# An AdaLN block whose query projection becomes three split products, with GpSimd and VectorE making the low halves

## What is computed

```python
mod = (_silu(L0_c) @ L0_wmod).reshape(L0_c.shape[0], 6, 1, -1)
sa, ca, ga, sb, cb, gb = (mod[:, 0], ..., mod[:, 5])
ga = (2 * (ga >= 0) - 1) * jnp.maximum(jnp.abs(ga), 0.25)        # gb alike
h = _layernorm(x, axis=-1) * (1 + ca) + sa
Q = jnp.einsum('bsh,hd->bsd', h, Wq) + bq                         # K = V = Q
scores = jnp.einsum('bqh,bkh->bqk', Q, K) / jnp.sqrt(128)
x = x + ga * jnp.einsum('bqk,bkh->bqh', softmax(scores), V)
h = _layernorm(x, axis=-1) * (1 + cb) + sb
# route = sigmoid(h @ Wr + br); out = max(route) * gelu(h @ W1[e]) @ W2[e], e = argmax(route)
x = x + gb * ffn(h)
```

## Time and profile before

| | us |
|---|---|
| median of 3 timed runs | 354.4 (354.29 to 354.92) |
| the profiled execution, device time | 354.34 |
| its span in the profile | 352.6 |
| busy share of the span | PE 92%, DVE 79%, ACT 63%, POOL 55% |
| attention slots 3 to 12 | 11.75 each |
| attention slots 1, 2, 13, 14 | 11.89, 12.61, 13.50, 12.96 |

### The profile page before, as it was taken

How to read it: one execution, slowest core, us unless ns; L and a number is a source line. 1 busy time by engine, 2 the same in 40 slices (tenths; PEclk the granted TensorE clock), 3 DMA queues, 4 the chain that set the end, 5 groups by cost and what they waited for, 6 DMA issues and landing times.

```text
span 352.6 us, 8419 instructions
## 1 busy us (share of the span) xinstructions
PE 325.0 (92%) x2578; PEld 299.6 (85%) x2578; DVE 278.9 (79%) x1114; ACT 223.5 (63%) x477; POOL 193.1 (55%) x224
## 2 busy tenths in 40 slices
PE   2799999999999999999989898899999999999960
PEld 2388788889888988898878798899999999999960
DVE  5378898898889888988997896899897777877730
ACT  2589987888788878887866585654445454434320
POOL 5016467545754575457525445877566556565661
PEclk9999999999999999999999999999999999999995
DMA  3394124337653666943536612664989554454300
GB/s 113 116 256 104 44 68 131 100 112 121 146 105 104 123 128 188 249 138 111 105 91 224 231 50 87 186 205 134 289 259 307 166 171 120 127 139 125 93 21 4
DMA packets 34493, 49.27 MB, mean 140 GB/s; under 512 B 4320, under 2 KB 26115, under 8 KB 34448
## 3 DMA queue, kind: packets, MB, share of 16 engines
q1 hardware_dynamic: 27504, 31.74, 37.0%
q0 software_dynamic: 6368, 16.92, 12.9%
q10 hardware_dynamic: 576, 0.07, 0.1%
HBM read 28.21 MB, written 20.96 MB: 139 GB/s over the span
## 4 chain that ended last, share of the span: by engine, by line
PE 70%; DVE 13%; ACT 6%; issue 5%; DVEq 2%; DMA 1%; POOL 1%; POOLq 0%; SPq 0%; ACTq 0%
PE mixed L625 14%; PE mixed L525 12%; PE flipped L512 6%; PE side L479 4%; PE scores L502 3%; PE scores L500 3%; PE scores L501 3%; PE side L545 3%; PE side L469 2%; PE scores L609 2%; PE scores L610 2%; PE scores L608 2%; PE side L537 2%; PE side L487 2%; PE flipped L609 2%
## 5 line engine op out<-in xcount | busy, mean ns | idle before, releaser
L1406 POOL DMA_INDIRECT sorted_rows<-payload,slots x64 | 63.9, 998 | 79.8 <-DVE slots L1044 64.9
L1433 POOL DMA_INDIRECT out_dram<-y_out,tokens x71 | 74.9, 1055 | 42.4 <-DVE y_out L1105 25.8
L625 PE MATMUL mixed<-down_slot,hidden 128*128 128x128 f32 x568 | 70.1, 276 | 2.5 <-ACT hidden L804 2.5
L625 PEld LDWEIGHTS mixed<-down_slot,hidden 128*128 128x128 f32 x568 | 66.5, 192 | 3.0 <-ACT hidden L804 3.0
L525 PE MATMUL mixed<-v_sb,probs_t 128*128 128x128 f32 x512 | 69.0, 278 | 0.0
L747 ACT ACTIVATE probs<-scores,row_max 128x512 f32<-128x512 f32 x64 | 44.0, 687 | 35.1 <-DVE row_max L937 33.4
L525 PEld LDWEIGHTS mixed<-v_sb,probs_t 128*128 128x128 f32 x512 | 62.2, 192 | 0.2
L937 DVE TENSOR_REDUCE row_max<-scores 128x1 f32<-128x512 f32 x64 | 44.1, 688 | 19.0 <-PE scores L502 19.0
L789 ACT ACTIVATE f_hi<-side 128x256 fp32r<-128x256 f32 (+1 forms) x39 | 14.3, 366 | 42.8 <-PE side L587 42.8
L512 PE MATMUL flipped<-ident,probs 128*128 128x128 f32 x256 | 39.1, 275 | 0.4 <-ACT probs L747 0.3
L755 ACT ACTIVATE probs_t<-flipped 128x512 f32<-128x512 f32 x64 | 37.9, 594 | 0.0
(11 more groups left out here) (187 smaller groups left out, 768.7 us busy)
## 6 DMA issues: line engine op xcount, KB each, us to landing
rows<-sorted_rows SPq DMA_DIRECT2D x32, 388.0 KB, 3.7
x_tile<-in_L_attn_inputs_dram SPq DMA_DIRECT2D x16, 256.0 KB, 3.2
payload<-stored_gates SPq DMA_DIRECT2D x16, 256.0 KB, 9.3
sorted_rows<-pad_rows SPq DMA_DIRECT2D x9, 388.0 KB, 4.6
w_parts<-in_L_ffn_W_dram SPq DMA_DIRECT2D x1, 2048.0 KB, 8.8
rows<-sorted_rows SPq DMA_DIRECT2D x7, 194.0 KB, 2.6
out_dram<-y_out,tokens POOLq DMA_INDIRECT x71
gate<-stored_gates SPq DMA_DIRECT2D x16, 64.0 KB, 5.8
```

What stands on the lines that cost most here:

```text
L625: last = nc.tensor.matmul(mixed[t % 2][:, u * H:(u + 1) * H], hidden[:, t % 2, f, u * P:(u + 1) * P], down_slot[:, t % 3, f, :], start=(f ...
L1406: nc.gpsimd.indirect_dma_start(rows_dram, bass.IndirectOffsetOnAxis(ap=slots[:, c:c + 1], axis=0), payload[:, b.q, j, :], None).then_inc(s ...
L1433: nc.gpsimd.indirect_dma_start(out_rows, bass.IndirectOffsetOnAxis(ap=tokens[:, t % RING, u:u + 1], axis=0), y_out[:, t % RING, u, :], Non ...
```

## The change

- `project` no longer takes h_t and wq_sb. ScalarE's `input_t` writes h_hi, which is scale * xn rounded to fp32r, without the shift. A new `split_h` on VectorE reads the same PSUM bank and makes h_lo = scale * xn - h_hi. TensorE then adds three fp32r products: wq_lo with h_hi, wq_hi with h_lo, wq_hi with h_hi.
- The halves of Wq are made once: wq_hi by ScalarE, wq_lo by VectorE. The shift is multiplied with Wq once for all batches (a small float32 product of 16 columns into mixed0) and becomes part of q_bias, one column for each batch, made by VectorE.
- Both outputs of `query` now have the factor ROOT and the same bias, so q_lo = q_t - q_hi is a plain subtraction. It moves from VectorE to GpSimd, as the first step of GpSimd's slot, for all batches but the first, which VectorE does in slot -1 (`split_first_q`). V, which is made from q_t, is put right by a factor 1/ROOT in the gates; for this two of the four gate instructions of the start are each written as two of half the width.
- In TensorE's slot `project(after)` moves behind `score(now, 2)`. In VectorE's slot `split_h(after)` is second, right behind `find_max(now, 1)`, and `split_q(after)` is gone from its place in front of `find_max(now, 3)`.

```diff
@@ TensorE
-                pe.wait_ge(h_ready, b.n + 1)
                 if b.n == 0:
                     pe.wait_ge(s_small, 64)
-                nc.tensor.matmul(side[1][:], wq_sb[:], h_t[:], start=True, stop=True).then_inc(q_projected, 1)
+                    pe.wait_ge(s_dve0, 3)
+                    nc.tensor.matmul(mixed[0][:, 0:B], wq_sb[:], shift1[:], start=True, stop=True
+                                     ).then_inc(bias_product, 1)
+                    pe.wait_ge(wq_split, 1)
+                pe.wait_ge(h_split, b.n + 1)
+                nc.tensor.matmul(side[1][:], wq_lo[:], h_hi[:], start=True, stop=False)
+                nc.tensor.matmul(side[1][:], wq_hi[:], h_lo[:], start=False, stop=False)
+                nc.tensor.matmul(side[1][:], wq_hi[:], h_hi[:], start=False, stop=True).then_inc(q_projected, 1)
...
                 mix(before, 3)
+                score(now, 2)
                 project(after)
                 if ending:
                     flip_rows(0)
-                score(now, 2)
@@ ScalarE
+            act.wait_ge(s_small, 64)
+            nc.scalar.activation(wq_hi[:], wq_sb[:], ACT.Copy).then_inc(wq_half, 1)
...
-                nc.scalar.activation(h_t[:], side[1][:], ACT.Identity, bias=shift1[:, col],
-                                     scale=scale1[:, col]).then_inc(h_ready, 1)
+                nc.scalar.activation(h_hi[:], side[1][:], ACT.Identity, scale=scale1[:, col]).then_inc(h_ready, 1)
...
-                nc.scalar.activation(q_t[:, b.p, :], side[1][:], ACT.Identity, bias=bq_sb[:, 0:1]
+                col = slice(b.n, b.n + 1)
+                nc.scalar.activation(q_t[:, b.p, :], side[1][:], ACT.Identity, bias=q_bias[:, col], scale=ROOT
                                      ).then_inc(q_ready, 1)
@@ VectorE
+            dve.wait_ge(wq_half, 1)
+            nc.vector.tensor_sub(wq_lo[:], wq_sb[:], wq_hi[:].bitcast(F32)).then_inc(wq_split, 1)
+            dve.wait_ge(bias_product, 1)
+            nc.vector.tensor_scalar(q_bias[:], mixed[0][:, 0:B], bq_sb[:, 0:1], ROOT, ALU.add, ALU.mult
+                                    ).then_inc(bias_ready, 1)
+            def split_h(b):
+                dve.wait_ge(h_ready, b.n + 1)
+                nc.vector.scalar_tensor_tensor(h_lo[:], side[1][:], scale1[:, col], h_hi[:].bitcast(F32),
+                                               ALU.mult, ALU.subtract).then_inc(h_split, 1)
...
                 find_max(now, 1)
+                split_h(after)
                 residual(before, 2)
...
-                split_q(after)
+                if k == -1:
+                    split_first_q()
@@ GpSimd
+            def split_q(b):
+                if not real(b) or b.n == 0:
+                    return
+                pool.wait_ge(q_hi_ready, b.n + 1)
+                nc.gpsimd.tensor_sub(q_lo[:, b.p, :], q_t[:, b.p, :], q_hi[:, b.p, :].bitcast(F32)).then_inc(q_split, 1)
...
             def slot(k):
+                split_q(after)
                 invert1(after2)
                 invert2(before)
                 token_ids(before2)
```

More of the change, by code:

```diff
@@ L85, in adaln_block @@
         bq_sb = sb("bq_sb", [P, 1])
-        bq_root = sb("bq_root", [P, 1])
+        q_bias = sb("q_bias", [P, B])
+        wq_hi = sb("wq_hi", [P, H], F32R)
+        wq_lo = sb("wq_lo", [P, H], F32R)
         wr_sb = sb("wr_sb", [P, E])
@@ L122, in adaln_block @@
         xn = sb("xn", [P, J, H])
-        h_t = sb("h_t", [P, J * P])
+        h_hi = sb("h_hi", [P, J * P], F32R)
+        h_lo = sb("h_lo", [P, J * P], F32R)
         q_t = sb("q_t", [P, 2, J * P])
@@ L237, in adaln_block @@
         xn_flipped = sem("xn_flipped")
+        wq_half = sem("wq_half")
+        wq_split = sem("wq_split")
+        bias_product = sem("bias_product")
         h_ready = sem("h_ready")
+        h_split = sem("h_split")
         q_projected = sem("q_projected")
@@ L729, in query @@
                 if b.n == 0:
-                    act.wait_ge(s_small, 64)
+                    act.wait_ge(bias_ready, 1)
                 wait(act, q_split, b.n - 1)
                 wait(act, v_ready, b.n - 1)
-                nc.scalar.activation(q_t[:, b.p, :], side[1][:], ACT.Identity, bias=bq_sb[:, 0:1]
+                col = slice(b.n, b.n + 1)
+                nc.scalar.activation(q_t[:, b.p, :], side[1][:], ACT.Identity, bias=q_bias[:, col], scale=ROOT
                                      ).then_inc(q_ready, 1)
-                if b.n == 0:
-                    act.wait_ge(bias_ready, 1)
-                nc.scalar.activation(q_hi[:, b.p, :], side[1][:], ACT.Identity, bias=bq_root[:, 0:1], scale=ROOT
+                nc.scalar.activation(q_hi[:, b.p, :], side[1][:], ACT.Identity, bias=q_bias[:, col], scale=ROOT
                                      ).then_inc(q_hi_ready, 1)
@@ L1416, in slot @@
             def slot(k):
-                before2, before, after2 = batch_at(k - 2), batch_at(k - 1), batch_at(k + 2)
+                before2, before, after, after2 = (batch_at(k + d) for d in (-2, -1, 1, 2))
+                split_q(after)
                 invert1(after2)
```

20 lines of the change are left out of this document (11 added, 9 removed).

## The result

The changed kernel takes **359.67 us** (median of 4 runs, 359.07 to 359.81), the kernel before 354.54 beside it (4 runs): a ratio of 1.0137, 95% interval 1.012 to 1.0153. It is 5 us slower. The forecast of 355.7 and its range up to 358.6 missed; the time is near that of Rival 2 (359.2). The profiled execution took 359.58 us with a span of 357.8, against 352.6 before.

A forecast was written before the change was run, and what follows sets the result against it. TensorE bounds ten slots of 11.75 us; after the change a loop through GpSimd and VectorE takes over. 354.34 + 0.6 (start) + 1.0 (slots 1 and 2) + 0.0 (ten slots) - 0.2 (end) = 355.7 us, range 353.4 to 358.6.

The forecast's parts named there:

- Rival 2: VectorE's `var` is held while GpSimd subtracts: 0.35 us a slot, +3.5 over ten slots, 359.2 us in all; chance 0.10.
- TensorE's slot without another bound: Steady slots 3 to 12: three fp32r products replace the float32 projection, so TensorE's slot falls by 0.18 to 11.58 us.
- Loop through GpSimd: Steady slots: `slots`, scatter, split, powers, normalize2 and back grow from 10.76 to 11.76 us, giving back TensorE's whole gain.
- `var` held, ten slots: VectorE in slots 3 to 12: no hold of `var` by GpSimd's subtraction, so 0; +3.5 us if held.
- Split on GpSimd: GpSimd's 128x512 subtraction for q_lo takes 1.28 us, like L1412, with bounds 1.01 and 1.56.
- h_lo on VectorE, start to start: VectorE's new h_lo takes 0.60 us, within 0.55 and 0.75, and stands on no binding path.
- Slots 1 and 2: GpSimd is already late there, so rstd2 comes later: +0.6 and +0.4, together +1.0 us, bounds 0 and +1.8.
- Start: First projection waits for VectorE's gates, wq_lo, q_bias and h_lo, ending at 14.3: +0.6 us, bounds +0.2 and +1.2.
- Slot 13: Full on VectorE with the same count of instructions: zero change.
- Slot 14: TensorE's saving reaches `find_max`: -0.2 us.
- the forecast case: GpSimd's loop sets the steady slot, within 0.08 us of 11.76: 355.7 us, own range 354.8 to 356.9; chance 0.45.

The follow-up runs named there:

- low parts on VectorE: Changed kernel with all q_lo made by VectorE again, in front of find_max(now, 3); 354.63 us against 354.66 for the kernel before, ratio 0.9997.
- reduction: Changed kernel with `var` written as a sum over one element instead of an addition, EPS left out of the second norm; 356.61 us, ratio 1.0046.
- the repetition: The changed kernel measured once more with nothing altered; 359.56 us against 354.66 for the kernel before, ratio 1.013.
- split in the middle: Changed kernel with GpSimd's order altered to second norm's power, q's subtraction, first norm's power; 365.52 us, ratio 1.0301.
- split last: Changed kernel with GpSimd's order altered to second norm's power, first norm's power, then q's subtraction; 368.91 us, ratio 1.0404.
- the altered start: Wq's low part made earlier, first projection into a free bank: 369.4 us with GpSimd's subtraction behind both powers, 354.28 us with q_lo and h_lo on VectorE.

## Why the prediction was wrong, step by step

| Step | Forecast | Measured |
|---|---|---|
| TensorE's slot without another bound | 11.58 us | 11.61 (low parts on VectorE) |
| Loop through GpSimd | 11.76 | 11.77 (reduction) |
| `var` held, ten slots | 0 (Rival 2: +3.5) | 120.46 - 117.74 = +2.7 |
| Split on GpSimd | 1.28 | 1.29 |
| h_lo on VectorE, start to start | 0.60, on no binding path | 0.65; slot 13 gets longer |
| Slots 1 and 2 | +1.0 | +0.99; -0.09 without the split |
| Start | +0.6 | +1.04; +1.55 in the repetition |
| Slot 13 | 0 | +0.48 |
| Slot 14 | -0.2 | -0.38 |

From the forecast to the profiled execution 3.8 us are missing: 2.7 are `var`, 0.5 slot 13, 0.4 the start, and small terms of both signs the rest. That Rival 2's 359.2 lies so near is in part luck: its hold was sized at 0.35 us a slot and measured 0.28, and the start and slot 13 made up for that.

**The failed step** is in the choice between the forecast case and Rival 2, where the prediction took it that `var` stays clear of GpSimd's subtraction: "The point from which it decides is the order of those two starts." The two starts were placed well. Measured from the slot's first `find_max`, `var` was to start at 4.7 and starts at 4.69, the split at 4.8 to 5.0 and starts at 4.86. So `var` does start first, by 0.17 us, and is held all the same, in nine slots of ten at 0.16 to 0.19 us ahead and in slot 3 at 0.32. That the order of the two starts decides was the error: the hold that the prediction put at nothing is 1.3 us on `var` and 0.28 us a slot. The row of a free `var` is 0.17 us long; this one would have ended just as the other began. A margin of 0.1 to 0.3 us on a wait of 1.3 us deserved more than a chance of 0.10, the more so as each slot repeats the same meeting. One can also see why the meeting is stable: the split starts 4.87 us behind the scatter, the scatter 0.29 behind `slots`, and `slots` hangs on the VectorE queue that `var` holds.

The trace of before had shown it, and I read only q_lo's 1.72 us there. `var` itself, free 0.17 us, took 0.97 us in slot 1 and 0.63 in slot 2, where it starts inside one of the L1412 subtractions, and ended with it both times (34.69 and 45.64; the subtractions end at 34.66 and 45.61). VectorE and GpSimd, before:

```profile
33.72 0.97 DVE L972 TENSOR_SCALAR var<-moments 128x4 f32<-128x4 f32 x1
...
45.01 0.63 DVE L972 TENSOR_SCALAR var<-moments 128x4 f32<-128x4 f32 x1
```
```profile
32.14 2.52 POOL L1412 TENSOR_TENSOR w_parts<-w_parts 128x512 fp32r<-128x512 f32 x2
```

A rule that I had applied to q_lo and h_lo alone bears on the small instructions as well. The Trainium skill (GPSIMD Engine Reference, section 8, Key points) names two kinds of VectorE instructions that contend with GpSimd, those in a 2-port mode and those with two SBUF inputs. By that rule, rows agree for `at_max`, with two SBUF inputs (held, 1.28 us), and for instructions with an input in PSUM: `v_sb` takes 0.69 us inside a subtraction, and h_lo 0.74 in each slot, also in slots 1 and 2, where it runs into one. `var` and `logit_d` have one SBUF input and are held (1.51 and 1.09 us); they fit only if they ran in a 2-port mode, which no trace here shows. Another sentence of the Trainium skill does not fit (SBUF — State Buffer, section "SBUF: two separate sides"): it says that the one that starts first gets the port pair for its whole instruction. By the rows the later one, GpSimd, won; it may be that the rows do not begin where the port is asked for, which no run here shows.

**Slots 1 and 2** came out as worked. `normalize2` in slot 1 waits 1.39 us for rstd2, and came just in time before. With the split back on VectorE the whole +1.0 is gone, which fits this reason.

**The start** has the right first part: h_lo starts at 11.80 (forecast 12.0) and q_t at 14.33 (14.3), 0.52 later than before; the prediction's own 14.3 less 13.77 is 0.5, which its sum took as 0.6. The other half microsecond was not in the sum: TensorE kept its slower pace longer, as the last section tells. In the repetition h_lo itself starts at 12.28, so half a microsecond at the start differs between executions of one kernel.

**Slot 13** was taken as full on VectorE and therefore at zero, "with the same count of instructions". The count is the same, but q_lo went from behind `find_max(now, 2)` and h_lo came in ahead of it: `find_max(now, 2)` comes 4.23 us behind the slot's first mark in place of 3.34, and only 0.4 of these 0.89 us come back up to `find_max(now, 3)`. Of the 0.89 us, 0.65 are h_lo. The other 0.24 are `full_i` of the early plan, 0.39 us where it took 0.15: shifted by h_lo, it now falls into the tail of a scatter issue and ends with it. VectorE and GpSimd, after:

```profile
178.76 0.39 DVE L1144 TENSOR_SCALAR full_i<-early_i 1x8 int32<-1x8 int32 x1
```
```profile
178.22 0.96 POOL L1439 DMA_INDIRECT sorted_rows<-payload,slots  x1 [0.30 <-issue]
```

**Slot 14** gave a little more than forecast.

What stays open: how near GpSimd's start a VectorE instruction may stand. `var` is held where its row starts 0.16 to 0.34 us ahead of the subtraction's, and clear at 1.3 us ahead (split in the middle). In the run with the split in the middle `var` starts 0.79 to 0.81 us behind the last scatter issue, as in the changed kernel, but a power follows and no subtraction, and it takes 0.17 us: the issue alone does not hold it there. But `ranked` (L1041, two SBUF inputs), 0.05 to 0.08 us ahead of the subtraction when that comes last, takes its free 0.17 us, and `at_max` 0.02 us behind the subtraction's start took 0.18 once (split in the middle), 1.28 at 0.03 behind once (split last). So the start of a row does not tell the moment that decides. For `var` and `ranked`, GpSimd's instruction in front is a scatter issue in the one case and a small product in the other; whether that is the difference was not tried.

## What to carry to other kernels

Before a wide elementwise instruction is moved to an idle GpSimd, list every VectorE instruction that will run beside it, small ones first: an addition, multiplication or comparison from SBUF to SBUF can stand still for the whole of it, and all of VectorE's queue with it; a reduction, a reciprocal or a layer norm's statistics from SBUF did not here. If it starts within a few tenths of a microsecond ahead, reckon with the hold, and look whether the same instruction has met a GpSimd instruction before in the trace that you have. Idle time of an engine inside a loop is not room; cost the loop with the new instruction in it, and ask of each new place which deadline it meets on the other side.

## What the hardware showed that I had not expected

- **Which VectorE forms were held beside GpSimd's 1.3 us subtraction, by the rows.** Held to its end: additions and comparisons of 4 or 32 columns from SBUF to SBUF (`var` 1.51, `logit_d` 1.09, `at_max` 1.28 us against 0.16 to 0.18 free). `mask`, which begins inside the subtraction when that comes last, takes 0.47, and `normalize2`'s 128 columns took 1.29 there once, in slot 2 (0.34 free). Not held: reductions (`var` as a sum 0.16, `find_max` 0.69), the reciprocal of 2 columns (0.15), the statistics of the second norm (0.29), and `v_sb`, whose other input is in PSUM (0.69). In the run with the subtraction last, `at_max` and the reciprocal behind it, VectorE and GpSimd:

```profile
191.72 1.28 DVE L1036 TENSOR_TENSOR at_max<-logit_d,least_d 128x32 f32<-128x32 f32 x1
192.93 0.17 DVE L1039 RECIPROCAL payload<-least_d 128x4 f32<-128x4 f32 x1
```
```profile
191.70 1.27 POOL L1420 TENSOR_TENSOR q_lo<-q_t,q_hi 128x512 fp32r<-128x512 f32 x1
```

- **A scatter issue holds such an instruction too, for a part of its 0.96 us.** In the timelines of slots 3 to 13 of seven kernels (before, after, and five of the experiments), an addition, multiplication or shift of 4 or 8 columns on VectorE (`var`, `neg_mean`, `full_i`) that starts 0.53 to 0.75 us behind the start of an issue, with no subtraction behind that, ends 0.92 to 0.94 us behind it, whatever its start; one that starts at up to 0.52, or from 0.76 on, takes 0.15 to 0.18 us (one at 0.38 took 0.20). The 512 columns of q_lo on VectorE, 0.68 to 0.72 us behind an issue, take their usual 0.68. The 0.33 us of `var` in the earlier trace rows was such a hold already, in the trace of before.
- **GpSimd's own duration hardly changes** (1.26 to 1.30 us in the changed kernel); the loser is VectorE. The other way round it does change: the 4-column power of the first norm, which runs beside VectorE's q_lo, is 1.55 us (median) with all low parts on VectorE, 1.05 in the changed kernel.
- **TensorE's pace at the start.** The granted clock reads 1.00 in each stretch from 5 us on, but products of 512 columns begin 0.43 us apart at first (1.2 columns per ns, the level of 1.2 GHz) and 0.23 apart later (the level of 2.4). The pace rose at about 18.5 us before, 18.9 with all low parts on VectorE, 20.0 in the changed kernel, and about 21.6 in its repetition. In the run with the altered start TensorE idled for 0.57 us in between and the pace rose at about 21.2. I put half of the changed kernel's loss at the start down to that, since the scores of row block 1 were still at the slower pace: from q_t to the first `find_max(now, 1)` it takes 5.92 us, and 5.40 before. What sets the moment of the rise, these runs do not show. The scores of row block 1, after:

```profile
18.61 0.78 PE L513 MATMUL scores<-q_hi,q_lo 128*128 128x512 f32 x1
19.19 0.63 PE L514 MATMUL scores<-q_lo,q_hi 128*128 128x512 f32 x1
19.61 0.59 PE L515 MATMUL scores<-q_hi 128*128 128x512 f32 x1
```

and with all low parts on VectorE:

```profile
18.85 0.51 PE L513 MATMUL scores<-q_hi,q_lo 128*128 128x512 f32 x1
19.20 0.40 PE L514 MATMUL scores<-q_lo,q_hi 128*128 128x512 f32 x1
19.44 0.40 PE L515 MATMUL scores<-q_hi 128*128 128x512 f32 x1
```
